# Second layer: the two halves of the normalised rows made in place and turned by DMA transfers instead of TensorE, rows of a block laid out 128 apart, loops written out

## The reference

```python
xn = _layernorm(x)                      # (x - mean) / sqrt(var + 1e-5), over the 128 channels
s = _L0_attn_ref(xn, ...)               # RWKV-like: k, v, r products, two scans over time
g = _silu(_L0_ffn_ref(xn, ...))         # three layers of +-1 weights, 512 wide
x = x + s * g
xn = _layernorm(x)
s = _L1_attn_ref(xn, ...)               # product with W_in, causal conv, silu, W_x, softplus step, scan, W_out
g = _silu(_L1_ffn_ref(xn, ...))         # 2 shared and 16 routed experts of 64 (gelu), top 4 gates from a softmax
return x + s * g
```

## Time and profile before

| | us |
|---|---|
| median of 3 runs | 686.22 (683.71 to 689.05) |
| the profiled execution, its own time | 683.87 |
| its span | 682.1 |
| PE busy, DVE busy, ACT busy, POOL busy | 630.9, 630.7, 506.7, 280.0 |

### The profile page before, as it was taken

One profiled execution on the slowest core, in us unless ns is written; L12 is line 12 of the kernel. 1 busy time (PEld: TensorE's weight loads), 2 busy tenths in 40 slices (PEclk: granted clock), 3 DMA queues, 4 the chain that ended last, 5 costly groups with the idle time before them and its releaser, 6 DMA issues. The chain is left out here.

```text
span 682.1 us, 10868 instructions
## 1 busy us (share of the span) xinstructions
PE 630.9 (93%) x2714; PEld 301.5 (44%) x2714; DVE 630.7 (92%) x1470; ACT 506.7 (74%) x808; POOL 280.0 (41%) x275
## 2 busy tenths in 40 slices
PE   4779999999999997889999999999999999999985
PEld 2334444444444443444444444444444444444442
DVE  4999999999999999989999999999999999999866
ACT  2846666666666665887887888888789788888874
POOL 6557777777676765133122212303303221230220
PEclk9999999999999999999999999999999999999999
DMA  7331000000000000000000000000000000000000
GB/s 174 106 94 31 0 1 0 0 0 0 0 0 0 0 0 0 1 1 0 17 17 0 16 15 0 16 15 0 15 15 15 0 15 15 0 15 15 0 16 31
DMA packets 10739, 11.29 MB, mean 17 GB/s; under 512 B 4800, under 2 KB 6288, under 8 KB 10720
## 3 DMA queue, kind: packets, MB, share of 16 engines
q1 hardware_dynamic: 9744, 10.73, 5.3%
q0 software_dynamic: 112, 0.33, 0.1%
q10 hardware_dynamic: 864, 0.00, 0.1%
HBM read 6.87 MB, written 4.19 MB: 16 GB/s over the span
## 5 line engine op out<-in xcount | busy, mean ns | idle before, releaser
L1177 PE MATMUL bank<-arena,w 128*128 128x512 f16 x640 | 148.6, 379 | 4.0 <-DVE arena L788 4.0
L1177 PE MATMUL bank<-arena,dnT 128*128 128x512 f32 x288 | 138.6, 592 | 0.0
L662 ACT ACTIVATE arena<-bank,xinv 128x512 f32<-128x512 f32 x144 | 94.8, 688 | 37.7 <-PE bank L1177 37.5
L444 POOL TENSOR_TENSOR arena<-arena 128x512 f32<-128x512 f32 x48 | 59.7, 1273 | 135.5 <-ACT arena L599 135.5
L1177 PEld LDWEIGHTS bank<-arena,w 128*128 128x128 f16 x640 | 62.5, 98 | 78.2 <-issue 10.0
L491 ACT ACTIVATE arena<-bank 128x512 f16<-128x512 f32 x96 | 53.9, 607 | 35.6 <-PE bank L1177 35.6
L434 POOL TENSOR_TENSOR arena<-arena 128x512 f32<-128x512 f32 x16 | 16.8, 1051 | 151.6 <-DVE arena L1025 151.6
L1177 PEld LDWEIGHTS bank<-arena,dnT 128*128 128x128 f32 x288 | 53.7, 191 | 35.9 <-issue 21.2
L1177 PE MATMUL bank<-arena,wsqT 128*128 128x512 f32 x128 | 64.5, 608 | 4.7 <-DVE arena L797 4.7
L1034 DVE SCALAR_TENSOR_TENSOR arena<-bank,cws,arena 128x506 f32<-128x506 f32 (+1 forms) x96 | 67.0, 740 | 1.1
L788 DVE SCALAR_TENSOR_TENSOR arena<-bank,arena 128x512 f16<-128x512 f32 x96 | 60.2, 670 | 2.4 <-ACT arena L491 1.2
(11 more groups left out here) (223 smaller groups left out, 1497.7 us busy)
## 6 DMA issues: line engine op xcount, KB each, us to landing
x_all<-in_L_attn_x SPq DMA_DIRECT2D x16, 256.0 KB, 2.6
out<-x_all SPq DMA_DIRECT2D x16, 256.0 KB, 2.0
up_n<-in_L_ffn_routed_up SPq DMA_DIRECT2D x1, 512.0 KB, 4.0
dn_n<-in_L_ffn_routed_down SPq DMA_DIRECT2D x1, 512.0 KB, 5.6
wx<-in_L_attn_W_x SPq DMA_DIRECT2D x1, 288.0 KB, 2.8
k_u<-in_L_ffn_k POOLq DMA_DIRECT2D x1, 256.0 KB, 5.7
w_in<-in_L_attn_W_in SPq DMA_DIRECT2D x1, 256.0 KB, 2.7
k_u<-in_L_ffn_k SPq DMA_DIRECT2D x1, 128.0 KB, 6.6
```

Source lines behind the costliest of these rows:

```text
L444: g.tensor_tensor(prod[:, c, :], act[:, c + 1, :], gate[:, :], ALU.mult).then_inc(sem["b_actp"], 1)
L662: a.activation(act[:, c, :], q_U[(c + 1) % 2][:, :], ACT.Gelu, scale=xinv[:, I_UP:I_UP + 1]).then_inc(sem["b_act"], 1)
L1177: return nc.tensor.matmul(ps, lhsT, rhs, start=start, stop=stop)
```

## The change

- `xn` of blocks 1 to 15 in the second layer is no longer transposed by PE. ACT writes the high half of `xn` as it stands (rows on partitions) to a new tile `xrh` (`rows_high`), DVE the low half to `xrl` (`rows_low`), and SP issues eight DMA transfers with transposition, 128x128 of float16 each, from these to `xh` and `xl` (or `xh_`, `xl_`). Block 0 still goes the old way.
- `rows_high` stands on ACT behind `high_xc(0)` and ahead of the two `logarithm`; `turned_high` behind `gelu(5)` is gone. `rows_low` stands on DVE behind the residual sum and ahead of `scan_input`; `turned_low` at the end of the pass is gone. The four transposes behind `expert_in(1)` on PE are gone.
- `conv_in(0)` waits on PE for the two DMA semaphores, all eight transfers.
- A block in SBUF now has row 128j + p in place j of partition p. A load or store of a block moves pieces of 512 B instead of 2 KB, and what was read or written in PE's transposes and the router's weight loads with a step of 4 elements (`j::J`) is now contiguous.
- The hardware loops are written out, with constants in all waits.

```diff
-    x_d = A["L0_attn_x"].rearrange("b t c -> (b t) c").rearrange("(g p j) c -> g p (j c)", p=P, j=J)
+    x_d = A["L0_attn_x"].rearrange("b t c -> (b t) c").rearrange("(g j p) c -> g p j c", p=P, j=J)
...
         def paired(eng, body):
 
-            for n in range(3):
-                body(n, n % 2)
-            with eng.Fori(0, (G - 4) // 2) as i:
-                body(2 * i + 3, 1)
-                body(2 * i + 4, 0)
-            for n in range(G - 1, G + 2):
+            for n in range(G + 2):
                 body(n, n % 2)
...
+            def turned(n):
+
+                for half, src, done in ((xh, xh_), xrh, "b_xhT"), ((xl, xl_), xrl, "b_xlT"):
+                    sp.wait_ge(sem["b_xrh" if src is xrh else "b_xrl"], n)
+                    after(sp, sem["b_up"], UC * (n - 1))
+                    for j in range(J):
+                        sp.dma_start(half[n % 2][:, j * P:(j + 1) * P], src[:, j * P:(j + 1) * P],
+                                     transpose=True).then_inc(sem[done], 16)
+
+            for n in range(G + 2):
+                if has(n + 1):
+                    turned(n + 1)
+                if has(n - 2):
+                    store(n - 2)
...
+            def rows_high(n):
+
+                actv.wait_ge(sem["b_xn"], n + 1)
+                after(actv, sem["b_xhT"], 16 * J * (n - 1))
+                a.activation(xrh[:, :], xn[:, :, :].rearrange("p j c -> p (j c)"), ACT.Copy, scale=XS).then_inc(sem["b_xrh"], 1)
...
                     high_xc(0)
+                    if has(f + 1):
+                        rows_high(f + 1)
                 if has(m):
                     logarithm(0)
                     logarithm(1)
...
                     for c in range(2, UC):
                         gelu(c)
-                        if c == 5 and has(f + 1):
-                            turned_high(f + 1, 1 - par, q_D[1])
...
+            def rows_low(n):
+
+                dve.wait_ge(sem["b_xrh"], n)
+                after(dve, sem["b_xlT"], 16 * J * (n - 1))
+                v.scalar_tensor_tensor(xrl[:, :], xn[:, :, :].rearrange("p j c -> p (j c)"), XS, xrh[:, :], ALU.mult,
+                                       ALU.subtract).then_inc(sem["b_xrl"], 1)
...
                     v.tensor_tensor(xs_of(t), xs_of(t), q_Q[:, :], ALU.add).then_inc(sem["b_out"], 1)
+                if ahead:
+                    rows_low(f + 1)
...
-                if ahead:
-                    turned_low(f + 1, 1 - par, q_D[1])
...
                 if has(f):
-                    pe.wait_ge(sem["b_xl"], f + 1)
+                    if f == 0:
+                        pe.wait_ge(sem["b_xl"], 1)
+                    else:
+                        pe.wait_ge(sem["b_xhT"], 16 * J * f)
+                        pe.wait_ge(sem["b_xlT"], 16 * J * f)
                     conv_in(0)
...
-                    if has(f) and has(f + 1) and c == 1:
-                        pe.wait_ge(sem["b_xn"], f + 2)
-                        if isinstance(n, int) and n == 0:
-                            pe.wait_ge(sem["a_x1"], G)
-                        after(pe, sem["b_cr"], IC * (m + 1))
-                        turn_rows(q_D[1]).then_inc(sem["b_xnT"], 1)
```

More of the change, by code:

```diff
@@ L292, in peeled @@
                     between[n]()
-            for n in range(3):
-                peeled(n)
-            with eng.Fori(3, G - 1) as n:
-                body(n)
-            for n in range(G - 1, last):
+            for n in range(last):
                 peeled(n)
         def paired(eng, body):
-            for n in range(3):
-                body(n, n % 2)
-            with eng.Fori(0, (G - 4) // 2) as i:
-                body(2 * i + 3, 1)
-                body(2 * i + 4, 0)
-            for n in range(G - 1, G + 2):
+            for n in range(G + 2):
                 body(n, n % 2)
@@ L539, in layer0 @@
                     a.activation(thr[:, :], b_RX[:, :], ACT.Tanh, scale=0.5).then_inc(sem["a_thr"], 1)
-                    if not (isinstance(f, int) and f == 0):
+                    if f != 0:
                         high(0, f, 0)
@@ L750, in normalised @@
                 dve.wait_ge(sem[ph + "rstd"], n + 1)
-                after(dve, sem[ph + "xnT"], n)
+                if ph == "b_" and n > 1:
+                    dve.wait_ge(sem["b_xrh"], n - 1)
+                else:
+                    after(dve, sem[ph + "xnT"], n)
                 for j in range(J):
@@ L852, in layer0 @@
                     last.then_inc(sem["a_scanV"], 1)
-                if has(f) and not (isinstance(f, int) and f == 0):
+                if has(f) and f != 0:
                     low(0, f, 0)
@@ L1143, in layer1 @@
                     gates(f)
[L1144 removed]
+                if n == 0:
                     matrices()
@@ L1187, in turn_rows @@
                 for j in range(J):
-                    last = nc.tensor.transpose(ps[:, j::J], xn[:, j, :], ident[:, :])
+                    last = nc.tensor.transpose(ps[:, j * P:(j + 1) * P], xn[:, j, :], ident[:, :])
                 return last
```

108 lines of the change are left out of this document (53 added, 55 removed).

## The result

The kernel with the change takes **698.38 us** (median of 4 runs, 695.17 to 699.24); the kernel before, run beside it, 685.76 us (683.71 to 689.05). The ratio is 1.0171, with a 95% interval of 1.0118 to 1.0224: 12.6 us slower, where 10.7 were forecast (696.9 us). The profiled execution of after took 697.58 us with a span of 695.7; before it was 683.87 and 682.1, so 13.6 us of span are to be explained.

What follows compares the result with a forecast made beforehand. A closed chain of waits through DVE, ACT and PE was taken to bound the kernel: 683.87 + 7.4 + 3.2 - 0.5 + 0.6 = 694.6, plus 2.3 for the median, gives 696.9 us (chance 0.60), range 686 to 740.

Steps and rivals of the forecast that it cites:

- ACT's `rows_high`: Added copy between `high_xc(0)` and the logarithms, where ACT has no idle: 0.53 us in 14 passes, +7.4 us.
- turn from pass 0 to 1: PE's `conv_in(0)` of pass 1 waits once for the late low half's transfers: 0.8 to 5.7 us, taken as +3.2.
- loops and layout: Written-out loops save 0.08 us at each of six turns, -0.5 us; contiguous access on PE gives 0.
- pieces of 512 B: First load and last store cost 0.3 us more each with smaller pieces: +0.6 us, bounds 0 to 1.6.
- the ring: Second layer's closed chain of waits from DVE's `sg` through ACT's `gelu(0)`, PE's `expert_in` and ACT's `ffn_silu`: 24.47 us.
- The break-even: At `conv_in(0)`, the eight transfers stay hidden up to 1.65 us per transfer; they were taken as hidden.
- rival A: Transfers not hidden, so `conv_in(0)` waits for them each pass: 697 to 744 us, chance 0.25.
- Rivals B: Not slower: ACT idle absorbs `rows_high` and PE's removed transposes come back as time: 683.5 us, chance 0.11.
- C: Transfers turn the data element by element, not in blocks: about 1,000 us more over 14 passes, chance 0.04.
- Gain 0: Removing PE's four transposes ahead of `expert_in(2)` only lengthens PE's wait for `gelu(0)`: 0 us.
- Cover holds by 0.12 us. Cost 0: DVE's earlier `rows_low`, at 0.67 us, delays `output` to 436.58, before PE reaches w_out at 436.70: 0 us.
- Contiguous access: 0: Contiguous access of transposes and router weights acts on PE, off the chain that sets the period: 0 us.

Runs made afterwards that it cites:

- experiment 1: Kernel before, plus one ACT float16 copy of the normalised rows in the second layer, which nothing reads; PE still turns the rows: 693.61 us, ratio 1.0093.
- experiment 2: Changed kernel without DMA transposes: new row layout and written-out loops, but PE turns the rows: 685.22 us, ratio 0.998.
- experiment 11: Changed kernel with only `rows_low` moved later, behind `scan_input(1)`: 697.28 us, ratio 1.0170.
- experiment 3: Changed kernel with `rows_low` for block 1 written ahead of the weight preparation on DVE, in pass 0 alone: 694.85 us, ratio 1.0114.
- experiment 4: Changed kernel with the high half's four transfers issued a second time, to a tile nobody reads, ahead of the low half's: 747.31 us, ratio 1.0879.
- first: Changed kernel with `high_xc(0)` moved behind `gelu(1)` and DVE's caps moved earlier: 712.12 us, ratio 1.0385.
- third: Kernel with new layout and written-out loops but PE turning the rows, plus `high_xc(0)` behind `gelu(1)` and caps earlier: 688.21 us, ratio 1.0022.
- fourth attempt: Changed kernel with GpSimd writing both halves, `high_xc(0)` behind `gelu(1)` and caps earlier: 700.66 us, ratio 1.0219.
- second attempt: Changed kernel with `high_xc(0)` behind `gelu(1)`, caps earlier, and `rows_low` later, behind `scan_input(1)`: 701.68 us, ratio 1.0231.
- 9: The third attempt's kernel, PE turning the rows, with DVE's caps moved behind `output_weight(0)`: 679.91 us, ratio 0.9909.
- 10: Changed kernel with high half on DVE, low half on GpSimd, `high_xc(0)` and caps later, next `conv_in(0)` ahead of w_out, `expert_out(4)` later: 687.13 us, ratio 1.0020.

## Why the prediction was right, and where its terms were off

The parts add up. Period before 24.42, `rows_high` +0.52 (experiment 1), layout and loops -0.11 (experiment 2): 24.83, and experiment 11 has 24.82. `rows_low` beside GpSimd adds 0.13: 24.95. So the period that had been forecast to the hundredth was met **by two errors that cancel**, and that is luck. Over the two profiled executions:

| term | predicted | measured | from |
|---|---|---|---|
| ACT's `rows_high` | +7.4 | +7.3 | experiment 1: 0.5 up to the first `sg`, 13 x 0.52 |
| turn from pass 0 to 1 | +3.2 | +4.7 | 5.03 of after, less 0.50 and plus 0.17 of experiments 1 and 2; 0.6 of it lies ahead of the wait (experiment 3) |
| DVE's `rows_low` | 0 | +1.7 | 13 x 0.13 (experiment 11 against after) |
| loops and layout | -0.5 | -2.1 | 13 x 0.11 and 0.2 up to the first `sg` (experiment 2), 0.4 in the first layer |
| pieces of 512 B | +0.6 | +0.4, not resolved | first `sg` of the first layer 0.32 later; the end, 0.03 |
| eight transfers | 0 | 0 | land 2 us early in each pass but the first |
| last pass | none | +1.7, the execution's own | 19.91 against 18.25 |
| sum | +10.7 | +13.7 | span +13.6 |

The term for the pieces is not resolved, because the first `sg` moves by more than that between executions: it comes at 39.78 in before and 41.80 in experiment 1, both with pieces of 2 KB, and between 40.10 and 42.73 in the traces with 512 B.

**Right, and shown.** What bounds the kernel (the ring, by experiment 1), that PE's freed work is worth nothing in the passes behind (24.83 us by experiments 1 and 2, which have the transposes, and 24.82 in experiment 11, which has not), that pass 0 absorbs its `rows_high` (`s1W` comes 12.18 us behind the first layer's last `sg` in before and in experiment 1), that the transfers are hidden in all passes but the first of them, and that pass 1 waits for the low half. The break-even was put at 1.65 us per transfer; it is 1.23, so rival A was nearer than the "three times the issue step" made it look: the nearest rows, plain small transfers at 0.46 us, were a bad measure. The other estimate in that step, from VectorE: DVE Perf Modes of the Trainium skill (The three transpose paths), took its 1309 ns as the step in the queue; with 11.3 us in all against a measured 433.31 to about 444.9 it was the better one. Rivals B and C did not happen.

**The turn from pass 0 to 1 was mis-sized**, as 3.2 in place of 4.7. The transfers' share was within its bounds (4.92 us for four issues and 2.4 to land, 7.3; the bounds were 3.5 and 8.4). What the step left out was the price on both sides of the wait. *Ahead* of it, the transposes' "Gain 0" does not hold in pass 0: with them gone and `gelu(0)` later PE waited 2.46 us in one piece, its clock fell, and `s1W` came 0.6 us late (experiment 3). *Behind* it, `conv_in(0)` starts 3.3 us later than before (295.95 against 292.65), DVE's maximum 4.5 us later (299.08 against 294.59): 1.2 us more, since the products between them run 0.43 us apart instead of 0.22. The prediction had no term for the clock at all.

**"Cover holds by 0.12 us. Cost 0" was wrong**, with a small price. The duration of `rows_low` was taken from an instruction of the same shape that had stood elsewhere, at the end of the pass. At its new place it has a neighbour. GpSimd's timeline in after, in pass 1 and in the pass shown above:

```profile
310.59 1.42 POOL L439 TENSOR_TENSOR arena<-arena 128x512 f32<-128x512 f32 x1 [9.51 <-DVE arena L1045]
...
435.37 1.04 POOL L439 TENSOR_TENSOR arena<-arena 128x512 f32<-128x512 f32 x1 [9.51 <-DVE arena L1045]
```

In the later pass GpSimd's instruction runs from 435.37 to 436.41, and `rows_low` from 435.81 to 436.96: it ended 0.55 us behind GpSimd's end, where it takes 0.68 alone, so it was held until about then. In pass 1 `rows_low` came first, at 310.43; it took 0.68 us, and GpSimd's instruction 1.42 in place of 1.04. SBUF — State Buffer of the Trainium skill (SBUF: two separate sides) describes just this, a pair of ports that the two engines share as a lock held for the whole instruction, by which a DVE operation with two SBUF inputs blocks against one of GpSimd that reads SBUF, as L439 does; the trace agrees, and the prediction should have asked for it where it gave the cover as 0.12 us.

**"Contiguous access: 0" was a little off in the other direction**, -0.11 us per pass together with the loops, for which the step had -0.04.

**The last pass is not the change's.** In the seven traces with the same order of instructions there, the last interval goes with PE's granted clock in it: 18.25 us at 1.00 in before, 18.22 at 1.00 in experiment 11, 18.73 at 0.97 in experiment 1, 19.10 at 0.95 in experiment 2, 19.15 at 0.95 in experiment 3, 19.43 at 0.93 in experiment 4, 19.91 at 0.91 in after. So these 1.7 us belong to the execution, and of the 13.6 us of span 11.9 are left for the change. In the runs of before, too, the time goes roughly with the mean clock (683.8 us at 0.999, 685.3 at 0.996, 689.0 at 0.989 to 0.992, but 686.0 at 0.990). So the medians' 12.6 us need not be the change's alone either.

**Missed altogether** were the expectations for the first, third and fourth attempt. Each took the ring as the bound and named a rival, a second ring or GpSimd, that was to cost no more than 2 us in all (first and third) or 1 us a pass (fourth, 693 us); measured were 13.7 us over the changed kernel, 3.0 over experiment 2, and 700.66 us. With 0.6 us taken off the first ring, the one through w_out and the router product was the longer, and moving the caps up had made it longer still. The second attempt's 0.68 us came as expected, its period did not (25.16 for 24.45). The two experiments behind them, 9 and 10, take the second ring into account: 9 came out 3 us better than expected. 10 missed its range by 4 us, and not by what its expectation had named for such a time, a period of 24.4 and more. Against experiment 2, whose trace begins alike, its 13 periods give 2.1 us back, the turn from pass 0 to 1 costs 3.1 and the last interval 1.8 (20.88 us, at a granted clock of 0.97; its order of instructions there is another). What sets its period of 24.14 is not shown.

## What to carry to other kernels

Taking work from an engine pays only where that engine closes the ring that sets the period; follow the waits around once, and once more for the ring that closes next, with its slack, before an instruction is moved. What replaces the work has its place too: one small ACT instruction in the wrong place cost 7.3 us here, while four transposes on PE had cost nothing, and where `gelu(0)` came later as well, taking them away joined two short waits of PE into a long one, with the low clock behind it. A duration read from one place holds at another only if the neighbours are the same: look up what GpSimd does at the new place whenever a DVE instruction reads only SBUF (with two inputs, or with one as the caps), and put DVE work that reads PSUM beside GpSimd.

## What the runs showed of the hardware

- Transposing transfers of 128x128 float16 from SBUF to SBUF leave SP's queue one every 1.23 us (plain ones 0.46) and land 2.4 us after issue. They overlap: eight take some 11.6 us, not eight landings.
- A DVE instruction with two inputs in SBUF, started beside one of GpSimd's, takes 1.15 instead of 0.68 us; two of them 2.41 instead of 1.41. DVE's caps, with one input in SBUF, took 1.73 instead of 0.95 us for two. Of `rows_low` and GpSimd's L439, whichever came first took its own time (0.68, 1.04), and the other was held (1.15, 1.42). DVE instructions with an input in PSUM were not slowed (1.41 for two beside GpSimd's 1.16).
- A float16 copy of the 128x512 normalised rows costs 0.61 us on ACT, 0.43 on DVE (tensor_scalar) and 1.59 on GpSimd, beside DVE.
- After PE's wait of 2.62 us for the transfers, its products ran at 0.43 us apart with a granted clock of 0.74 over 10 us. That added 1.2 us to the wait's price by the time of the DVE maximum. The wait of 2.46 us for `gelu(0)` in pass 0 was followed by the low level too, a wait of 1.44 us at the same place in experiment 1 was not, and in experiment 4 seven waits of 2.4 to 2.6 us were not either.
